# Recurrent block with banded relative attention and routed experts: expert tiles gather, finish and scatter their own rows; band and strip are turned and copied inside one step

## What is computed

```
xn = layernorm(x)                                  # x: 2 x 2048 x 256, float32
q, k, v = xn @ W.T + b, 16 heads of 16
scores = (q.k + q.rel_k[clip(j - i, -128, 128) + 128]) / sqrt(16)
w = softmax(scores)
s = (w @ v + sum_j w[i, j] rel_v[clip(j - i, ...) + 128]) @ Wo.T + bo
e = argmax(xn @ Wg + bg)                           # one of 8 experts per token
y = gelu_tanh(xn @ W1[e]) @ W2[e]                  # 256 -> 1024 -> 256
out = x + s * silu(y)
```

## Time and profile before

| | before |
|---|---|
| time, median of 3 | 2706.46 us |
| profiled execution: time, span | 2709.98 us, 2707.9 us |
| PE busy | 2427.3 us (90%) |
| DVE, ACT, POOL busy | 1817.5, 1746.8, 798.7 us |
| DVE row maxima, L1088 | x2048, 590 ns each |
| ACT exponentials, L1150 | x2048, 525 ns each |
| DMA | 548.10 MB, mean 202 GB/s |

### The profile page before, as it was taken

The page is one execution under the profiler, slowest core; times in us unless marked ns, Lnnn a source line. Parts: engine busy times, 40 slices in busy tenths (PEclk is TensorE's granted clock), DMA queues, the critical chain, the costliest instruction groups (busy, mean ns, idle before and its releaser), DMA issues. The chain is left out here.

```text
span 2707.9 us, 48933 instructions
## 1 busy us (share of the span) xinstructions
PE 2427.3 (90%) x15216; PEld 1180.9 (44%) x15217; DVE 1817.5 (67%) x4947; ACT 1746.8 (65%) x3996; POOL 798.7 (29%) x1880
## 2 busy tenths in 40 slices
PE   6828999999999999999999999999999987999991
PEld 3402444444444444444444444444444444666661
DVE  6558777777777777777777777777777752322223
ACT  4514777777777777777777777777777774111111
POOL 1222333333333333333333333333333343000005
PEclk9956999999999999999999999999999998999996
DMA  6648777777777777777677767777777655300005
GB/s 215 194 147 269 227 220 235 237 219 229 239 233 229 233 240 233 220 235 239 217 225 233 235 217 235 238 229 231 236 240 228 213 177 211 123 31 31 31 29 190
DMA packets 364301, 548.10 MB, mean 202 GB/s; under 512 B 24640, under 2 KB 276528, under 8 KB 364080
## 3 DMA queue, kind: packets, MB, share of 16 engines
q1 hardware_dynamic: 356112, 526.45, 62.8%
q0 software_dynamic: 7968, 18.91, 2.3%
HBM read 270.73 MB, written 274.46 MB: 201 GB/s over the span
## 5 line engine op out<-in xcount | busy, mean ns | idle before, releaser
L1088 DVE TENSOR_REDUCE part<-ps 128x1 f32<-128x512 f32 (+3 forms) x2048 | 1188.4, 590 | 445.8 <-PE ps L972 433.7
L1150 ACT ACTIVATE probs_T<-pst 128x512 f32<-128x512 f32 (+3 forms) x2048 | 986.2, 525 | 395.0 <-PE pst L981 392.6
L972 PE MATMUL ps<-k_front,q_front 96*128 96x512 bf16 x2048 | 791.1, 393 | 12.4 <-DVE part L1086 2.1
L930 PE MATMUL pout<-probs_T,v_far 128*32 128x512 f32 (+3 forms) x4864 | 550.8, 533 | 40.8 <-ACT probs_T L1126 31.5
L843 POOL TENSOR_TENSOR left_T<-probs_T,left_mask 128x128 f32<-128x128 f32 x512 | 220.0, 430 | 987.3 <-ACT probs_T L1126 788.2
L972 PEld LDWEIGHTS ps<-k_front,q_front 96*128 96x128 bf16 x2048 | 198.9, 97 | 586.4 <-DVE part L1088 298.3
L981 PE MATMUL pst<-q_back,k_left 102*128 102x512 bf16 (+3 forms) x1024 | 350.0, 343 | 0.9 <-ACT probs_T L1150 0.6
L981 PE MATMUL pst<-q_back,k_right 102*128 102x512 bf16 (+3 forms) x1024 | 348.7, 342 | 0.4
L1163 ACT ACTIVATE band<-band,negm 128x384 f32<-128x384 f32 (+1 forms) x512 | 305.7, 597 | 0.1
L1086 DVE CUSTOM_DVE_ANT_0 band<-ps,band 128x256 f32<-128x256 f32 (+2 forms) x704 | 299.4, 425 | 0.0
L930 PEld LDWEIGHTS pout<-probs_T,v_far 128*32 128x32 f32 x4864 | 174.5, 108 | 238.3 <-issue 211.7
(11 more groups left out here) (156 smaller groups left out, 2191.0 us busy)
## 6 DMA issues: line engine op xcount, KB each, us to landing
rel_scores<-rel SPq DMA_DIRECT2D x128, 1024.0 KB, 7.9
band_probs<-band SPq DMA_DIRECT2D x128, 768.0 KB, 4.3
pwin<-band_probs SPq DMA_DIRECT2D x128, 512.0 KB, 5.8
band<-rel_scores SPq DMA_DIRECT2D x64, 768.0 KB, 6.6
band<-rel_scores SPq DMA_DIRECT2D x64, 576.0 KB, 5.4
w<-in_w_dram SPq DMA_DIRECT2D x16, 1024.0 KB, 12.7
band<-rel_scores SPq DMA_DIRECT2D x64, 128.0 KB, 6.0
q_terms<-terms SPq DMA_DIRECT2D x48, 128.0 KB
```

Source lines behind the costliest of these rows:

```text
L930: return nc.tensor.matmul(pout[32 * g:32 * g + 32, c0:c1], values, probs, start=first, stop=False, skip_group_check=True)
L972: nc.tensor.matmul(ps1[u % 2][:, :], q_front[a.par][:, a.s * P:(a.s + 1) * P], k_front[a.par][:, u * CW:(u + 1) * CW], start=True, stop=Tr ...
L1088: ins = nc.vector.tensor_reduce(peak, src, AX_X, ALU.max)
L1150: ins = nc.scalar.activation(probs_T[t.s % 2][:, u * CW + c0:u * CW + c1], pst[u % 2][:, c0:c1], ACT.Exp, scale=SCALE)
```

## The change

1. **attend, order of a step.** TensorE's transposes of band and strip move from behind part 4 to behind part 3 (u == 2), `turn_back` behind them; the first strip product moves from part 3 to part 1, the second from part 4 to part 3. VectorE's strip copy and ScalarE's band copy are now those of the same step: behind part 3 on both engines, where they were behind part 1, and first, of the step after.
2. **Slots instead of sorted rows.** No zeros and no `x_sorted`. In attend's first step POOL fills a table `slots` (39 x 128 pairs: row to write to, row to read), with padding rows beyond the output; in head 1 (units 2 and 3) it scatters the token numbers into it, one indirect DMA a step, and SP copies the rows of x into `x_and_s`, a table of 1 KB of x and 1 KB of attention result for each token. SP loads the table in head 2.
3. **experts.** All loops are unrolled. The projected attention rows go to `x_and_s` in groups of four tiles (a buffer for two groups, stored by POOL). For each tile POOL gathers the normalised rows, gathers x and s of its rows, and scatters the result to the output, with rings of three buffers. Behind the output product: tanh(y / 2) on ScalarE, three VectorE operations for x + s * y * (1 + tanh(y / 2)) / 2. The output tensor has padding rows, which are cut off at the end. Before the output weights have landed, the first tiles are already copied and turned.
4. **finish** is gone.

In the diff, `w` in the copies becomes `t`; the other waits are the same with new counts.

```diff
+RING = 3
+OUT_ROWS = (TILES + RING) * P
...
-                sp.wait_ge(zero_set, 1)
-                sp.dma_start(dram["xs"].rearrange("(t p) d -> p t d", p=P), zeros[:, :].unsqueeze(1).to_broadcast([P, XT, D])).then_inc(zeros_out, 16)
...
-                    tok = off - FIRST_ROW + 1
-                    if at_end(hb) and 0 <= tok < TILES and tok % GROUP == 0:
-                        k = tok // GROUP
-                        if k < 2:
-                            sp.wait_ge(rel_out[2 + k], NBH * 16)
-                        else:
-                            sp.wait_ge(sorted_out[k % 2], 16 * GROUP * (k // 2))
-                        sp.dma_start(rows[k % 2], xn_v[:, tok:tok + GROUP, :]).then_inc(row_in[k % 2], 16)
+                    if hb == 1 and off < TILES:
+                        sp.dma_start(dram["x_s"][off * P:(off + 1) * P, 0, :], x_tok[off * P:(off + 1) * P, :]).then_inc(x_copied, 16)
+                    if hb == 2 and off == 2:
+                        sp.wait_ge(slots_filled, 16 * TILES)
+                        sp.dma_start(slots[:, :, :], dram["slots"].rearrange("(t p) k -> p t k", p=P)).then_inc(slots_in, 16)
...
-                    tok = off - FIRST_ROW
-                    if at_end(hb) and 0 <= tok < TILES:
-                        k, slot = divmod(tok, GROUP)
-                        pool.wait_ge(row_in[k % 2], 16 * (k // 2 + 1))
-                        pool.indirect_dma_start(out=dram["xs"][:, :], out_offset=bass.IndirectOffsetOnAxis(ap=pos_i[:, tok:tok + 1], axis=0),
-                                                in_=rows[k % 2][:, slot, :], in_offset=None).then_inc(sorted_out[k % 2], 16)
+                    if at_start(hb) and off == 0:
+
+                        pool.iota(empty[:, :, 0].rearrange("p (a r) -> p a r", r=RING), pattern=[[0, XT // RING], [P, RING]], base=TILES * P,
+                                  channel_multiplier=1).then_inc(tok_set, 1)
+                        pool.iota(empty[:, :, 1], pattern=[[0, XT]], base=0, channel_multiplier=0).then_inc(tok_set, 1)
+                        for k in range(2):
+                            pool.iota(tok_i[:, :, k], pattern=[[P, TILES]], base=0, channel_multiplier=1).then_inc(tok_set, 1)
+                        pool.wait_ge(tok_set, 4)
+                        pool.dma_start(dram["slots"].rearrange("(t p) k -> p t k", p=P), empty[:, :, :]).then_inc(slots_set, 16)
+                    if hb == 1 and off < TILES:
+                        if off == 0:
+                            pool.wait_ge(slots_set, 16)
+                        pool.indirect_dma_start(out=dram["slots"][:, :], out_offset=bass.IndirectOffsetOnAxis(ap=pos_i[:, off:off + 1], axis=0),
+                                                in_=tok_i[:, off, :], in_offset=None).then_inc(slots_filled, 16)
...
+                    def turn_band_and_window():
...
+                        if u in (0, 2) and w.s == NB - 1 and w.valid:
+                            pe.wait_ge(winT_evac, w.count(16, 16))
+                            near_values(u // 2).then_inc(near_pv, 1)
+                        if u == 2 and t.valid:
+                            turn_band_and_window()
+                        if u == 2 and o.s == NB - 1 and o.valid:
+                            turn_back()
...
-                        dve.wait_ge(winT_mm, w.count(16, w.s + 1))
-                        if w.s == 0:
-                            wait(dve, near_pv, w.count(2, 0))
-                        if w.s == NB - CH:
-                            wait(dve, back_mm, w.count(1, 0))
-                            if Step(hb, off - LAG_T - 1 + NB).valid:
-                                dve.wait_ge(v_built, w.count(1, 2))
-                        nc.vector.tensor_copy(pwin_T[:, :, w.s * P:(w.s + 1) * P], pnear.rearrange("p (b c) -> p b c", b=2)).then_inc(winT_evac, 1)
+                        dve.wait_ge(winT_mm, t.count(16, t.s + 1))
...
-                        if u == 0 and w.valid:
+                        if u == 2 and t.valid:
                             window()
...
-                    if w.valid:
-                        near_keys()
...
+                        if u == 2 and t.valid:
+                            near_keys()
...
-                def store(T, h):
-                    sp.wait_ge(y_evac, T + 1)
-                    sp.dma_start(dram["ys"][bass.ds(T * P, P), :], ys[h][:, :]).then_inc(y_out[h], 16)
...
+                def fetch_x(T):
+                    if T < XT:
+                        wait(pool, x_tp, T - RING + 1)
+                        pool.indirect_dma_start(out=xs[T % RING][:, :], out_offset=None, in_=dram["xn"][:, :],
+                                                in_offset=rows_of(dram["xn"], T, 1)).then_inc(xs_in[T % RING], 16)
+
+                def fetch_x_s(T):
+                    if T < XT:
+                        wait(pool, out_done[T % RING], landed(T) - 16)
+                        pool.indirect_dma_start(out=xg[T % RING][:, :, :].rearrange("p k d -> p (k d)"), out_offset=None,
+                                                in_=dram["x_s"].rearrange("t k d -> t (k d)"),
+                                                in_offset=rows_of(dram["x_s"], T, 1)).then_inc(xg_in[T % RING], 16)
+
+                def put(T):
+                    pool.wait_ge(res_ready, T + 1)
+                    pool.indirect_dma_start(out=out[:, :], out_offset=rows_of(out, T, 0), in_=xg[T % RING][:, 0, :],
+                                            in_offset=None).then_inc(out_done[T % RING], 16)
+
+                for T in range(RING):
+                    fetch_x(T)
+                s_tab = dram["x_s"].rearrange("(t p) k d -> p t k d", p=P)
+                for g in range(TILES // SG):
+                    pool.wait_ge(s_ready, SG * (g + 1))
+                    pool.dma_start(s_tab[:, SG * g:SG * (g + 1), 1, :], s_rows[g % 2][:, :, :]).then_inc(s_out[g % 2], 16)
+                for i in range(2):
+                    pool.wait_ge(s_out[i], 16 * (TILES // SG // 2))
+                for T in range(RING - 1):
+                    fetch_x_s(T)
+                for T in range(XT):
+                    fetch_x(T + RING)
+                    fetch_x_s(T + RING - 1)
+                    put(T)
+                for i in range(RING):
+                    pool.wait_ge(out_done[i], 16 * (XT // RING))
...
+                for T in range(XT):
+                    e = pe.value_load(expert_i[0:1, T:T + 1], min_val=0, max_val=NE - 1)
                     for half in range(2):
-                        hidden(T, h, e, half)
-                        turn_hidden(T - 1, 1 - h, half)
-                    if next_count is not None:
-                        turn_x(T + 1, next_count, 1 - h)
-                    output(T - 1, 1 - h, e_before)
-
-                wait(pe, o_evac, TILES)
-                turn_x(0, 16, 0)
-                pe.wait_ge(w1_in, 16 * NE)
-                e0 = expert(0)
+                        hidden(T, e, half)
+                        if T > 0:
+                            turn_hidden(T - 1, half)
+                    if T + 1 < XT:
+                        turn_x(T + 1)
+                    if T == 1:
+                        pe.wait_ge(w2_in, 16 * NE)
+                    if T > 0:
+                        output(T - 1, e_before)
...
+                def tanh(T):
+                    act.wait_ge(y_mm, T + 1)
+                    wait(act, res_ready, T - 1)
+                    nc.scalar.activation(gate[T % 2][:, :], py[:, 0:D], ACT.Tanh, scale=0.5).then_inc(tanh_done, 1)
+
+                for T in range(XT):
+                    hidden(T)
+                    if T > 0:
+                        tanh(T - 1)
+                tanh(XT - 1)
...
+                    g = t // SG
                     dve.wait_ge(o_mm, t + 1)
-                    nc.vector.tensor_tensor(token_tile(t), heads(po[h][:, 0:D]), heads(bo[:, :]), ALU.add).then_inc(o_evac, 1)
-
-                dve.wait_ge(wo_in, 32)
+                    if t % SG == 0:
+                        wait(dve, s_out[g % 2], 16 * (g // 2))
+                    nc.vector.tensor_tensor(s_rows[g % 2][:, t % SG, :], po[h][:, 0:D], bo[:, :], ALU.add).then_inc(s_ready, 1)
...
-                def output(T, h, out_count):
-                    dve.wait_ge(y_mm, T + 1)
-                    wait(dve, y_out[h], out_count)
-                    nc.vector.tensor_copy(ys[h][:, :], py[:, 0:D]).then_inc(y_evac, 1)
...
+                def finish(T):
+
+                    g, r = gate[T % 2], T % RING
+                    dve.wait_ge(tanh_done, T + 1)
+                    nc.vector.scalar_tensor_tensor(g[:, :], g[:, :], 1.0, py[:, 0:D], ALU.add, ALU.mult).then_inc(y_used, 1)
+                    dve.wait_ge(y_used, T + 1)
+                    dve.wait_ge(xg_in[r], landed(T))
+                    nc.vector.scalar_tensor_tensor(g[:, :], g[:, :], 0.5, xg[r][:, 1, :], ALU.mult, ALU.mult).then_inc(gated, 1)
+                    dve.wait_ge(gated, T + 1)
```

(29 more changed lines are left out.)

297 lines of the change are left out of this document (98 added, 199 removed).

## The result

The changed kernel took **2721.82 us** in the median of five runs (2718.33 to 2723.0), where the kernel before took 2706.46 us beside it, also in the median of five. The ratio is 1.0053, with a 95% interval of 1.0041 to 1.0064. It is slower by half a per cent; the forecast was 37 us faster. The profiled execution has a span of 2720.1 us against 2707.9, so 12.2 us have to be found.

What follows compares the result with a forecast made beforehand. TensorE, or what it waits for, was taken to bound attend, in a 3.75 us ring through ScalarE's late band copy. Terms 31 + 5 - 7 + 1 - 5 + 3 - 14 - 51 = -37 gave 2669.5 us, range 2615 to 2705.

Steps and rivals of the forecast that it cites:

- The new ring: Attend step: strip transposes, VectorE's strip copy, fourth maximum, next second score product, then TensorE's products; base step 3.90 us.
- the attention term: Attend's new order makes a unit 64.4 us against 63.4, +31 us for 31 units, range -5 to +66.
- The last unit: Attend's last 16 steps, where VectorE has no maxima: 2.9 us a step on average, +5 us.
- Rival (a): Attend: VectorE doesn't close the new step; ScalarE's exponential ring of 3.66 us does, -119, about 2550 us; 10%.
- Rival (b): Attend: ScalarE's band copy delays the fourth exponential and the next second transposed product; slower, up to 2735 us; 10%.
- (c): Expert tiles: POOL's chain passes 8.1 us a tile; a landing of 5.7 us gives 2724; 4%.
- (d): The edit doesn't do what it says: loops still stall, zeros were not the wait; +21, 2690 us; 6%.
- Zeros: Project: without the 5 MB of zeros, VectorE's 6.76 us wait at 74.41 goes; -7, bounds -7 and 0.
- Fill: Slot table's fill and read, with the scatters and row copies added in attend: 0 to 8 us, taken as +1.
- The barrier: End of attend: POOL's last row scatter no longer holds the block until SP's first load; -5 us.
- the +0: Projection: with queues served round-robin, stores go beside weight loads and their term is +0, the total 4 us less.
- the estimate of 6.9 us a tile: Expert tiles: ScalarE's time of an 8.1 us tile if tanh and gelu were in different table sets; still hidden.

Runs made afterwards that it cites:

- band_same: Changed kernel with attend's old orders, except TensorE's band transposes behind part 3 and ScalarE's band copy ahead of its fourth exponential: 2645.2 us, ratio 0.9768.
- rel_after: Changed kernel with the relative scores' product moved behind the key-value product in the step behind the output's turn: 2712.1 us, ratio 1.0010.
- copy_last: Changed kernel with VectorE's strip copy behind the fourth maximum instead of ahead of it: 2699.1 us, ratio 0.9961.
- s_fine: Changed kernel with projection stores in groups of two tiles and four buffers instead of four tiles and two: 2725.9 us, ratio 1.0061.
- score_first: copy_last with TensorE's fourth score product issued ahead of the band and strip transposes: 2592.2 us, ratio 0.9578.

## Why the forecast was wrong

**The bound before** was read rightly only in part. The forecast found one step closed by ScalarE's late band copy, 3.75 us, and took it to be so "round and round". `band_same` moves that copy, and the 25.4 us wait went, but the unit fell only from 63.37 to 63.16: five of the 13 plain steps became 0.09 to 0.31 us shorter (that of 3.75 came to 3.44) and others up to 0.17 longer. The shift transposes' wait of 53 us was real, and went in the changed kernel. The 266 us, read there as the score products' wait for the maxima, are the weight load's; the idle time ahead of the products themselves was 5.9 us.

**The new ring, the step that failed.** The step that failed is the attention term, +31 us for 31 units: its mechanism was right and its size was not, +74 measured. The forecast found the right ring for the changed kernel: strip transposes, copy, fourth maximum, next second product. One turn in the changed kernel is 1231.02 (strip), 1231.44 (copy), 1231.78 (maximum), 1232.60 (product), 1234.25 (third product), 1235.02 (strip):

```profile
1231.02 0.38 PE L958 MATMUL psmall<-ident,pwin 128*128 128x128 f32 x2
...
1232.60 0.39 PE L991 MATMUL ps<-k_front,q_front 96*128 96x512 bf16 x1 [0.48 <-DVE part L1092]
...
1234.25 0.39 PE L991 MATMUL ps<-k_front,q_front 96*128 96x512 bf16 x1
...
1235.02 0.38 PE L958 MATMUL psmall<-ident,pwin 128*128 128x128 f32 x2
```

It is 4.00 where the base was put at 3.90, since the fourth maximum is split by the band here: 0.82 from its start to the product, against 0.74. On average over the 13 plain steps the forecast came to 3.86 and the trace to 3.93. The 0.07 lies half on VectorE's side (1.56 for 1.53) and half on TensorE's. That is 0.9 us of the 1.4 us by which the unit was missed. The step behind the output's turn is another 0.3: the forecast gave it only the four transposes, 4.23, and left out that VectorE's normalisation then stands behind the late maximum; `rel_after` shows it. The steps with strip products and left values are the last 0.2 (5.65 + 4.49 where about 9.9 was put). Over 31 units this is +74 for +31. The last unit, put at +5, came to +1: the last three turns of the output are 97.1 us apart where they were 96.1. The text named the lever (0.07 a step is 35 us) and its range reached to +66; both the size and the range of this one term failed. Its own sign of being wrong, a unit over 66, was too wide to show it: the unit was 65.75.

**What was overlooked** is larger than the miss. Rival (a) said that the next ring below is ScalarE's, at 3.66 us, and -119 us if VectorE's copy doesn't close the step. `copy_last` took the copy out of the path and gained 23. The next ring was VectorE's own, from the fourth product, at 3.80, because moving the transposes ahead of that product puts them inside it. The forecast costed the transposes as TensorE's work, in a sum, and not by which product is queued behind them. Rival (b) was right that the kernel could become slower than before, but not by its path: ScalarE's early copy was free (`band_same`), and from 260 to 2150 us no wait of a transposed score product for an exponential is listed in the changed kernel. (c) did not occur (TensorE was busy 312 of 315 us), and (d) only in that the zeros' wait came back later.

**The start.** Zeros: the forecast took the whole 6.8 us wait as the gain, the far end of its bounds; project is 0.6 us shorter in the profile and some 1.5 in the median of all, since a wait of the same kind took its place at 100.38. Fill: put at +1 in a range of 0 to 8, cost about 7 in this profile and 9 in the runs; the value was too low, as bytes were counted and not pieces, and the range of 0 to 8 barely had it. Together the start missed by 13 us, beside the 36 of attention.

**What held.** The barrier (-5.1 for -5). The expert tiles: no idle time at the loop's turn, TensorE busy 312 of 315 us, 16.6 us gained for 14 forecast (11.5 of it idle time, and 5.0 busy time, for which no run here has a reason); tanh and three operations of 0.42 stand in VectorE's idle time. The end, 7.4 us behind the last product where 5.6 was worked out:

```profile
2712.71 0.38 ACT L1390 ACTIVATE gate<-py 128x256 f32<-128x256 f32 x1 [5.98 <-PE py L1346]
2713.12 0.42 DVE L1437 SCALAR_TENSOR_TENSOR gate<-gate,py 128x256 f32<-128x256 f32 x1 [3.82 <-ACT gate L1390]
...
2714.04 0.42 DVE L1442 TENSOR_TENSOR xg<-gate,xg 128x256 f32<-128x256 f32 x1
2716.17 0.97 POOL L1273 DMA_INDIRECT out_dram<-xg,slots  x1 [6.81 <-issue]
```

The last scatter goes 1.7 us behind VectorE's last operation, where it is 0.3 in the tiles before; the trace gives no releaser. The projection came to +4.9 for +3, with the mechanism as forecast (the double buffer waits for landings). The cost was real: the first output product starts 61.8 us behind the stage's first load, where it was 57.0. But it isn't the waits' alone, as `s_fine` shows: beside the stores the last of the weights also landed later, 59.0 us behind the first load for 50.9. The Trainium skill's rule that was weighed there (DMA: Bandwidth & Descriptors, SWDGE vs HWDGE vs iDMA), that each DMA engine round-robins between the two queues, is not contradicted by this: both kinds went on side by side. What doesn't fit is the +0 that the forecast worked out from it. A store of 512 KB landed in 6.9 us in the median beside the loads, near the 9.0 of the loaded row, VectorE waited 4.0, 2.9 and 2.8 us for such landings, and the loads came 8 us later.

## What to carry to other kernels

When work is moved on an in-order engine, first write down the rings that pass through each point where it could stand, and ask which product is now queued behind it: 0.55 us of transposes cost 107 us ahead of the fourth score product (`copy_last` against `score_first`), and behind it no wait of a score product for its maximum is listed. Where the forecast multiplies a step by 496, a term of 0.07 us is the whole answer, so the range must be as wide as what the rows can't resolve. A removed wait counts as a gain only when the next thing that ends late is known: the zeros gave back most of theirs within project, and the stores' ring all of it. And a wait of the weight load is not yet a wait of the product: look for the PE row.

## What the runs showed of the hardware

A transfer of 39 KB as 4992 pieces of 8 bytes on POOL's queue left TensorE waiting 10 to 16 us for operands that SP's queue loaded at the same time; as 128 pieces of 312 bytes it left 2.5 to 3.0 us, as without the transfer (2.8 and 3.2). It landed after 18.9 to 23.9 us in the one form and 1.9 in the other, and took POOL itself 2.02 and 0.60 us to issue. (The numbers of pieces are those of the program's layout.)

ScalarE ran tanh and the expert's gelu by turns in every tile, with one table load in the whole stage:

```profile
L1385 ACT ACT_TABLE_LOAD x1 | 1.3, 1283 | 0.0
```

The Trainium skill (ScalarE: Activation LUTs, What ACT_TABLE_LOAD costs) counts 1.28 us of a switch for the load and 1.38 for the drain behind it. The trace agrees on the load (1283 ns); between gelu and tanh there is none, so the estimate of 6.9 us a tile in the forecast had nothing to apply to.
